# A four-layer kernel: the second batch's 50 rounds of balancing move from DVE to ACT and PE

## The reference

```python
def sinkhorn_log(logits, num_iters=50, tau=0.1):      # logits: one 4x4 matrix for each token
    Z = logits / tau
    def step(carry, _):
        u = -logsumexp(Z + v[..., None, :], axis=-1)
        v = -logsumexp(Z + u[..., :, None], axis=-2)
    (u, v), _ = scan(step, (0, 0), length=50)
    return exp(Z + u[..., :, None] + v[..., None, :])
...
H_res = (1 - g) * I + g * sinkhorn_log(H_res_logits)
x_mixed = einsum('btij,btjc->btic', H_res, x_streams)
ffn = x_mixed + y * softmax(H_post_logits)            # y = (x weighted by softmax(H_pre_logits)) @ W_branch
```

## Time and profile before

| | |
|---|---|
| median of 3 runs | 1462.56 us (1456.24 to 1465.91) |
| the profiled execution | 1467.78 us |
| its span in the trace | 1466.1 us |
| busy: PE / DVE / ACT / POOL | 1113.0 / 871.3 / 577.3 / 320.6 us |
| granted PE clock, mean | 0.868 |
| piece B + C + D + E | 155 + 125 + 125 + 156 us |

### The profile page before, as it was taken

How to read it: one execution, slowest core, us unless ns; L and a number is a source line. 1 busy time by engine, 2 the same in 40 slices (tenths; PEclk the granted TensorE clock), 3 DMA queues, 4 the chain that set the end, 5 groups by cost and what they waited for, 6 DMA issues and landing times.

```text
span 1466.1 us, 20210 instructions
## 1 busy us (share of the span) xinstructions
PE 1113.0 (76%) x7526; PEld 456.1 (31%) x7526; DVE 871.3 (59%) x1773; ACT 577.3 (39%) x785; POOL 320.6 (22%) x514
## 2 busy tenths in 40 slices
PE   2769999895788639746555457878788988898887
PEld 1444444342233314312312111222222233333332
DVE  4212222003666679886888988657758577746663
ACT  2413333000554435126113246574445555434452
POOL 1114444004841102001011043700010032111220
PEclk9869999997899859677776768998879999999999
DMA  3421220003210001100200111411002110210100
GB/s 130 144 87 45 85 65 22 0 0 94 65 29 18 12 1 55 34 6 20 62 13 22 56 53 36 138 29 31 17 27 74 50 32 23 77 54 28 53 18 29
DMA packets 53590, 67.14 MB, mean 46 GB/s; under 512 B 9494, under 2 KB 43412, under 8 KB 53488
## 3 DMA queue, kind: packets, MB, share of 16 engines
q1 hardware_dynamic: 49516, 55.95, 12.5%
q0 software_dynamic: 3984, 9.98, 2.4%
HBM read 46.82 MB, written 18.82 MB: 45 GB/s over the span
## 4 chain that ended last, share of the span: by engine, by line
PE 36%; DVE 31%; ACT 5%; issue 4%; SPq 1%; DMA 1%; ACTq 0%; DVEq 0%
DVE w_mx L1388 13%; PE w_banks L653 10%; PE w_po L1303 9%; PE w_banks L1285 4%; PE w_banks L1257 4%; DVE w_region L1875 3%; PE w_banks L1245 2%; ACT w_pr L1331 2%; DVE w_region L1872 2%; DVE w_region L1853 2%; DVE w_region L1870 2%; PE w_banks L1313 2%; PE w_banks L1539 1%; DVE w_region L1868 1%; DVE w_region L1866 1%
## 5 line engine op out<-in xcount | busy, mean ns | idle before, releaser
L1388 DVE TENSOR_REDUCE w_mx<-w_banks 128x2 f32<-128x1024 f32 (+3 forms) x352 | 377.1, 1087 | 195.6 <-PE w_banks L1257 194.0
L1331 ACT ACTIVATE w_pr<-w_banks 128x1024 f32<-128x1024 f32 (+1 forms) x312 | 315.1, 1013 | 429.3 <-PE w_banks L1285 427.9
L1370 POOL TENSOR_SCALAR_AFFINE_SELECT w_pr<-w_pr 128x512 f32<-128x512 f32 (+1 forms) x184 | 104.7, 569 | 561.5 <-ACT w_pr L1331 561.3
L1285 PE MATMUL w_banks<-w_qs,w_ks 49*128 49x512 f16 (+7 forms) x832 | 137.1, 354 | 91.1 <-DVE w_mx L1388 60.0
L1257 PE MATMUL w_banks<-w_ks,w_qs 48*128 48x512 f16 (+7 forms) x832 | 144.8, 361 | 40.9 <-DVE w_mx L1388 23.1
L1303 PE MATMUL w_po<-w_pr,w_vz 128*17 128x512 f32 (+7 forms) x1152 | 155.1, 565 | 12.7 <-ACT w_ou L1353 12.7
L78 PE MATMUL f_pp<-xt,sl_region 128*128 128x512 f16 x672 | 149.1, 382 | 3.5 <-POOL sl_region L492 3.5
L1245 PE MATMUL w_banks<-mask_half,ident_half 64*128 64x128 bf16 (+1 forms) x768 | 67.0, 254 | 37.2 <-DVE w_mx L1388 16.8
L78 PEld LDWEIGHTS f_pp<-xt,sl_region 128*128 128x128 f16 x672 | 65.1, 98 | 84.8 <-issue 5.6
L466 DVE TENSOR_TENSOR sl_region<-sl_region,f_pp 128x512 f32<-128x512 f32 x28 | 19.3, 688 | 121.3 <-ACT sl_region L481 121.3
L1285 PEld LDWEIGHTS w_banks<-w_qs,w_ks 49*128 49x128 f16 (+1 forms) x832 | 41.8, 99 | 138.9 <-issue 57.5
(11 more groups left out here) (223 smaller groups left out, 1533.6 us busy)
## 6 DMA issues: line engine op xcount, KB each, us to landing
stack_scratch<-sl_region SPq DMA_DIRECT2D x102, 128.0 KB
w_qs<-stack_scratch SPq DMA_DIRECT2D x96, 96.0 KB, 2.3
sl_region<-in_L_gu SPq DMA_DIRECT2D x14, 512.0 KB
w_stage<-in_L_w POOLq DMA_DIRECT2D x36, 128.0 KB, 2.4
sl_region<-in_L_down SPq DMA_DIRECT2D x14, 256.0 KB
stack_scratch<-p_qk SPq DMA_DIRECT2D x24, 128.0 KB
w_ks<-stack_scratch SPq DMA_DIRECT2D x32, 96.0 KB, 2.6
bw_stage<-in_L_w SPq DMA_DIRECT2D x4, 640.0 KB, 6.0
```

Of the source, the lines that this page charges most:

```text
L1285: mm = pe.matmul(g.banks.pair_at(f)[:, half, at:at + T - q0], g.ks[base:base + self.rows + 1, k_slot, k_place, j * P:(j + 1) * P], g.qs[ba ...
L1331: act.activation(g.probs.at(self.pr_fill[s])[:, :, 0:width], g.banks.pair_at(self.s_fill[s])[:, :, 0:width], ACT.Exp, scale=self.a.scale). ...
L1370: pool.affine_select(out=diagonal, in_=diagonal, compare_op=ALU.is_ge, fill=0.0, base=0, pattern=pattern, channel_multiplier=-1).then_inc( ...
L1388: dve.tensor_reduce(out, g.banks.pair_at(self.m_fill[m])[:, :, 0:heads * keys].rearrange("q h (p k) -> q h p k", k=keys), AX.X, ALU.max).t ...
```

## The change

`s1` becomes a `LogStreams`. The first batch's `s0` stays as it was. For `s1` the 64 columns are turned so that a partition is one of the 64 (tile, entry) pairs, for two halves of the tokens: `h_e` and `h_l` are 128 x 64. The logarithms of the matrices stay in a PSUM bank. A half round, of which there are 100, is four ticks: ACT takes exponents of the bank (L1965 in the new kernel, 128x64), PE multiplies them by a 128x128 table of ones, so that every entry gets the sum of its row or column (L1939, a single-precision matmul of 64 columns), ACT takes the logarithm of that (L1969, 128x64), and PE adds minus a tenth of it to the bank (L1943, the same size). 100 half rounds are 200 matmuls and 200 activations and one more exponent at the end; two transposes lead in and two lead out. Each tick waits for the one before. The bank of the logarithms and the one of the sums are held through the whole balancing; they are the first two of the seven, which is one pair.

After each Sqrt and each Silu the kernel now loads a table set that holds exponent and logarithm; the program has 35 table loads where it had 32, and none of them lies between the exponents and logarithms of the balancing.

The cuts between pieces move too. `s0` does 100 of its steps in piece B and 200 in piece C (before 180 and 120). `s1` does 10 half rounds in piece C (before 60 steps, which is 20 half rounds), 60 in piece D (before 240 steps and the mixing), and the last 30 with the mixing in piece E, ahead of what stood there: the output projection, norm and projections of batch 1 for layer 2 and the routed ffn now come behind the end of `s1` in the same strand. Line numbers of the new kernel are two higher than before up to the balancing.

```diff
...
         if t == 11:
             act.wait_ge(self.centred.sem, self.centred.at + 2)
-            act.activation(g.h_mix[:, :, :], g.h_mix[:, :, :], ACT.Exp, scale=self.INV_TAU).then_inc(self.exped.sem, 1)
-            act.activation(g.h_pp[:, :, :], g.h_pp[:, :, :], ACT.Exp).then_inc(self.exped.sem, 1)
+            self.exponents(act)
...
+class LogStreams(Streams):
+    def __init__(self, g, b, xn, w24, wb, base, gate, norm, weights, sums):
+        super().__init__(g, b, xn, w24, wb, base, gate, norm, weights)
+        self.sums = sums
+        s, self.halves = g.signals, 2 * self.ITERS
+        self.spread = s.take("h_spread", 1)
+        self.entries, self.totals = s.take("h_entries", self.halves + 1), s.take("h_totals", self.halves)
+        self.logs, self.taken = s.take("h_logs", self.halves), s.take("h_taken", self.halves)
+        self.gathered = s.take("h_gathered", 1)
+        self.gate_at = self.bal_at + 4 * self.halves + 2
+        self.mix_at = self.gate_at + 3
+        self.ticks = range(self.mix_at + NI * 4 + 1)
+    def rounds(self, signals):
+        return None
+    def plan(self, t):
+        super().plan(t)
+        banks = self.g.banks
+        if t == self.bal_at - 1:
+            self.fills["logs"] = banks.fill(self.entries, self.halves + 1, (self, self.gate_at - 2))
+            self.fills["totals"] = banks.fill(self.logs, self.halves, (self, self.gate_at - 4))
+        if t == self.gate_at - 1:
+            self.fills["back"] = banks.fill(self.done, 12, (self, self.gate_at + 1))
+    def pe(self, pe, t):
+        super().pe(pe, t)
+        g, banks = self.g, self.g.banks
+        if t == self.bal_at - 1:
+            pe.wait_ge(self.centred.sem, self.centred.at + 2)
+            banks.free(pe, self.fills["logs"])
+            for low in (0, 64):
+                mm = pe.matmul(banks.at(self.fills["logs"])[low:low + 64, 0:64],
+                               g.h_mix[low:low + 64, :, :].rearrange("p t n -> p (t n)"), g.ident[low:low + 64, low:low + 64],
+                               start=True, stop=True)
+            mm.then_inc(self.spread.sem, 1)
+            banks.free(pe, self.fills["totals"])
+        k, hop = divmod(t - self.bal_at, 4)
+        if 0 <= k < self.halves and hop == 1:
+            pe.wait_ge(self.entries.sem, self.entries.at + k + 1)
+            pe.matmul(banks.at(self.fills["totals"])[:, 0:64], self.sums[:, k % 2, :], g.h_e[:, :],
+                      start=True, stop=True).then_inc(self.totals.sem, 1)
+        if 0 <= k < self.halves and hop == 3:
+            pe.wait_ge(self.logs.sem, self.logs.at + k + 1)
+            pe.matmul(banks.at(self.fills["logs"])[:, 0:64], self.sums[:, 2, :], g.h_l[:, :],
+                      start=False, stop=True, skip_group_check=True).then_inc(self.taken.sem, 1)
+        if t == self.gate_at - 1:
+            banks.free(pe, self.fills["back"])
+            pe.wait_ge(self.entries.sem, self.entries.at + self.halves + 1)
+            for low in (0, 64):
+                mm = pe.matmul(banks.at(self.fills["back"])[low:low + 64, 0:64], g.h_e[low:low + 64, :],
+                               g.ident[low:low + 64, low:low + 64], start=True, stop=True)
+            mm.then_inc(self.gathered.sem, 1)
+    def exponents(self, act):
+        act.activation(self.g.h_pp[:, :, :], self.g.h_pp[:, :, :], ACT.Exp).then_inc(self.exped.sem, 2)
+    def act(self, act, t):
+        super().act(act, t)
+        g, banks = self.g, self.g.banks
+        k, hop = divmod(t - self.bal_at, 4)
+        if t >= self.bal_at and (k < self.halves and hop == 0 or t == self.gate_at - 2):
+            if k == 0:
+                act.wait_ge(self.spread.sem, self.spread.at + 1)
+            else:
+                act.wait_ge(self.taken.sem, self.taken.at + k)
+            act.activation(g.h_e[:, :], banks.at(self.fills["logs"])[:, 0:64], ACT.Exp, scale=self.INV_TAU)\
+                .then_inc(self.entries.sem, 1)
+        if 0 <= k < self.halves and hop == 2:
+            act.wait_ge(self.totals.sem, self.totals.at + k + 1)
+            act.activation(g.h_l[:, :], banks.at(self.fills["totals"])[:, 0:64], ACT.Ln).then_inc(self.logs.sem, 1)
+    def balance(self, dve, k):
+        pass
+    def weigh(self, dve):
+        g = self.g
+        dve.wait_ge(self.gathered.sem, self.gathered.at + 1)
+        dve.tensor_scalar(g.h_mix[:, :, :], g.banks.at(self.fills["back"])[:, 0:64].rearrange("p (t n) -> p t n", t=NI),
+                          g.h_gt[:, 1:2], None, ALU.mult).then_inc(self.done.sem, 1)
...
-        cut = s0.bal_at + 180
+        cut = s0.bal_at + 100
...
-        s1 = Streams(g, 1, sl[:, 1], w24, wb, base24[:, :], gate[:, :], n11, [])
+        s1 = LogStreams(g, 1, sl[:, 1], w24, wb, base24[:, :], gate[:, :], n11, [small.done()], sums)
         s1.begins_after = [(n11, n11.ticks[-1])]
-        cut1 = s1.bal_at + 60
+        cut1, cut2 = s1.bal_at + 40, s1.bal_at + 280
...
-               [some_of(s1, cut1, s1.ticks[-1] + 1)], [all_of(split2)]],
+               [some_of(s1, cut1, cut2)], [all_of(split2)]],
...
-        merge([[body_of(a20)], [all_of(o11), all_of(n21), all_of(p21), all_of(r20), lead_of(a21)], [all_of(split3)]],
+        merge([[body_of(a20)], [some_of(s1, cut2, s1.ticks[-1] + 1), all_of(o11), all_of(n21), all_of(p21), all_of(r20),
+                                lead_of(a21)], [all_of(split3)]],
...
+    at = np.arange(P)
+    out["sums"] = np.stack([at[:, None] // 4 == at // 4, (at[:, None] // 16 == at // 16) & (at[:, None] % 4 == at % 4),
+                            -0.1 * np.eye(P)], axis=1).astype(f)
```

More of the change, by code:

```diff
@@ L44 @@
 PR_UNITS = 6
+TABLES = "natural_log_exp_and_others"
 def wait_pos(eng, sem, value):
@@ L691, in act @@
             act.activation(self.g.sd[:, 1, :], self.g.sd[:, 0, :], ACT.Sqrt).then_inc(self.std.sem, 1)
+            act.preload_act_table_set(TABLES)
         c = t - 8
@@ L1674, in __init__ @@
         self.centred, self.exped = s.take("h_centred", 2), s.take("h_exped", 2)
-        self.balanced = s.take("h_balanced", 6 * self.ITERS)
+        self.balanced = self.rounds(s)
         self.pre, self.turned, self.hi, self.lo = s.take("h_pre", NI * 4), s.take("h_turned", 1), s.take("h_hi", 1), s.take("h_lo", 1)
@@ L1683, in __init__ @@
         self.fills = {}
+    def rounds(self, signals):
+        return signals.take("h_balanced", 6 * self.ITERS)
     def cost(self, t):
@@ L1762, in act @@
             op.then_inc(self.posted.sem, 1)
+    def exponents(self, act):
+        g = self.g
+        act.activation(g.h_mix[:, :, :], g.h_mix[:, :, :], ACT.Exp, scale=self.INV_TAU).then_inc(self.exped.sem, 1)
+        act.activation(g.h_pp[:, :, :], g.h_pp[:, :, :], ACT.Exp).then_inc(self.exped.sem, 1)
     def silu(self, act, pair):
@@ L1836, in dve @@
             dve.wait_ge(done.sem, done.at + 11)
-            dve.wait_ge(self.balanced.sem, self.balanced.at + 6 * self.ITERS)
-            dve.tensor_scalar(g.h_mix[:, :, :], g.h_mix[:, :, :], g.h_gt[:, 1:2], None, ALU.mult).then_inc(done.sem, 1)
+            self.weigh(dve)
         elif t == self.gate_at + 2:
@@ L1855, in dve @@
                                          op0=ALU.mult, op1=ALU.add).then_inc(self.mixed.sem, 1)
+    def weigh(self, dve):
+        g = self.g
+        dve.wait_ge(self.balanced.sem, self.balanced.at + 6 * self.ITERS)
+        dve.tensor_scalar(g.h_mix[:, :, :], g.h_mix[:, :, :], g.h_gt[:, 1:2], None, ALU.mult).then_inc(self.done.sem, 1)
     def balance(self, dve, k):
@@ L2037, in weave @@
     g.st, g.mv, g.sd = sb("st", [P, NI, 6], F32), sb("mv", [P, NI, 2], F32), sb("sd", [P, 3, NI], F32)
-    g.swap = sb("swap", [P, P], F32)
+    g.swap, sums = sb("swap", [P, P], F32), sb("sums", [P, 3, P], F32)
     g.rank = sb("rank", [P, 8], F32)
@@ L2055, in weave @@
     g.h_ss, g.h_rr, g.h_gt = (view(region, at, (n,), F32) for at, n in ((5872, 4), (5876, 4), (5880, 3)))
+    g.h_e, g.h_l = view(region, 5888, (64,), F32), view(region, 5952, (64,), F32)
     wo1, w24 = view(tables, 0, (2, 2, D), F16), view(tables, 1024, (2, KC, 24), F16)
@@ L2085, in weave @@
                                    (g.rank[:, :], ins["rank"].partition_broadcast(P)), (g.swap[:, :], ins["swap"]),
+                                   (sums[:, :, :], ins["sums"]),
                                    (col3[:, :], ins["L3_qk_bias"]), (v_row3[:, :], ins["L3_v_bias"].partition_broadcast(P)),
```

## The result

| | before | changed |
|---|---|---|
| median of the runs | 1464.24 us (1456.24 to 1467.43) | 1595.30 us (1592.96 to 1598.78) |
| ratio, 95% interval | | 1.0906 [1.0854, 1.0958] |
| profiled execution, span, mean clock | 1467.78, 1466.1 us, 0.868 | 1592.96, 1591.3 us, 0.828 |
| pieces B, C, D, E, F | 155, 125, 127, 154, 176 us | 139, 152, 157, 236, 172 us |

Pieces are measured here from the first of a stage's transposes (L968, now L970) to the next stage's. In the changed kernel these come late in piece E, so D ends with the 70th half round.

A forecast was written before the change was run, and what follows sets the result against it. DVE was taken to bound the balancing stretches, with the two-engine chain late next. Terms -10 + 20 + 5 + 19 + 48 = +82 us, set against the median 1462.6, gave 1545; predicted 1540 us, range 1475 to 1600.

The forecast's parts named there:

- The half round, 1.64 us: Four chain ticks: two activations of 0.22 us, two matmuls of 0.47, hand-overs of 0.10 and 0.03; bounds 1.0 and 2.3.
- Other work between its steps: Pieces D and E: PE's 58.5 us less 18.6 hidden plus 6 for ACT in D; attention ticks 24 us in E.
- Piece B, -10: 80 DVE steps, 23 us, leave piece B; PE then leads its second half; -9 us there, bounds 0 and -17.
- Piece C, +25: The 80 steps come to a stretch 87% DVE, +20 us (12 to 23); ten half rounds replace 60 steps, +5.
- Piece D, 144: 60 half rounds of 98 us plus PE's partly hidden other work and attention exponents: 144 us against 125, +19.
- Piece E, 73 + 31 + 100: 30 half rounds with 16 attention ticks 73 us, mixing 31, remaining attention ticks and other work 100: 204 against 156, +48.
- Queues, banks, table loads at nothing: POOL's splits in E, up to 8 us late, the held PSUM pair and three more table loads of 1.29 us: counted as nothing.
- Hiding (1): Rival: the chain hides beside other work and PE gets its full clock back, 1430 us; chance 0.08.
- A short matmul (2): Rival: matmuls of 0.23 to 0.30 us, most other work hidden, B and C cancelling, about 1465 us; chance 0.08.
- The low clock (3): Rival: PE mostly waits, so its clock stays low; half round 2.06 us, about 1605; chances 0.05 over 1600, 0.17 for 1565-1600.
- Alternating table sets (4): Rival: exponent and logarithm come from different table sets, costing 256 us in the balancing; chance under 0.01.
- The signs: Chain stretch 225 to 245 us, half rounds 1.64 apart; wrong if 1.1 or less, E's last third much under 100, C not growing.

The follow-up runs named there:

- experiment 1: Changed kernel with the second batch balancing on DVE as before, in the change's new places: 1484.85 us, ratio 1.014 against the kernel before.
- experiment 2: Changed kernel with its chain in places near the old ones, none in piece E: 1596.33 us, ratio 1.0907 against the kernel before.
- experiment 10: Changed kernel without the logarithm and subtraction of each half round, matrices unbalanced: 1500.40 us, ratio 1.0241 against the kernel before.
- experiment 7: Kernel before with two PSUM banks held unused through the second batch's balancing, which stays on DVE: 1467.77 us, ratio 1.0043.
- experiment 4: Kernel before with the second batch's 300 balancing steps left out, same written order: 1422.00 us, ratio 0.9722.

## Why the prediction was right, and where its sizes were off

- **Mechanism.** Right. DVE was relieved and what was late next was the chain (experiments 1, 2 and 10). The time, 1595, lies in the range, but only 5 us below its upper end, which was drawn for a half round of 2.2 us or the low clock. It is not in the 1490 to 1565 that had 0.62 but in the 1565 to 1600 that had 0.17. The forecast, 1540, was 55 us too low. Against the profiled execution's span it is +125 us where the sum had +82.
- **The half round, 1.64 us.** This term was too small. Without other work it was 2.00 us, with 0.69 for the matmul at the low clock, almost the 0.68 that the prediction had worked out for that clock. I took 0.47, "between the ends, because the clock of these pieces lies between". The mean was 0.60 (60.4 + 59.7 over 200). That is 26 us. The hand-over from ACT to PE was 0.06, not 0.10: 8 back. ACT's 0.22 was right. What I missed is that the clock would stay low although PE is busy 79% of the chain: I read 0.72 from a stretch in which PE did other things, and counted on a busier PE to raise it. The stretch from 716 to 740 ran at 0.50, all of it at 0.60, and the same places without a chain at 0.66 (experiment 1).
- **Other work between its steps.** 84 us of the 267, where the sum had 74 (238 less 164), at a clock of 0.72. In D it was 51 us (the sum: 58.5 - 18.6 + 6 = 46), in E 30 (24). The term for ACT was the one too small: in D its chain operations came 15 us late in all, where the sum had 6. Together the chain took 29 us more than the 21 + 144 + 73 of the sum.
- **Piece B, -10.** It was -16, at the good bound, with the clock at 0.94 in its second half instead of 0.84. **Piece C, +25.** It was +28: the head +20 as forecast, and 24 instead of 21 us for ten half rounds.
- **Piece D, 144.** It took 157. **Piece E, 73 + 31 + 100.** It took 86 + 35 + 115. The third part wasn't the chain's: experiment 1 has 119 there. PE had 85.2 us of work in it where I had 79.6, at a busy share of 75%. I had named 76% as one end and taken a value towards F's 85%; the stretch kept the share it had.
- **F unchanged.** 172 us against 176. **Queues, banks, table loads at nothing.** That was nearly so: the banks cost 6 us (experiment 7), the pair of loads inside the chain 2 us. The next activation began 1.29 us after the start of the second load, as in the earlier trace rows. The Trainium skill's drain of 1.38 us (ScalarE: Activation LUTs, "What ACT_TABLE_LOAD costs") is in neither. POOL's splits (60 us) found room in the third part.
- **The sum of the misses.** Chain +29, mixing +4, third part +15, B -6, F -4, pieces before B and after F +5: +43, which is 125 - 82.
- **The rivals.** Hiding (1) is refuted: without any second balancing the kernel gains 42 us (experiment 4), and the chain fills gaps only in the small. A short matmul (2) exists, in half precision, and gave the half round of 1.10 us; but the time fell to 1528, not 1465. The better clock and the better hiding that (2) counted on did not come: the clock was 0.59, and 100 half rounds took 200 us, not 110. The low clock (3) came true in part: a free half round of 2.00 us and a mean clock of 0.60. Its 1605 is nearer to the result than the forecast's 1540, and it deserved more than its 0.22. Its reason, that PE mostly waits, is not what the rows show: PE is busy 79% of the chain. Alternating table sets (4) did not come: one pair of loads in 200 activations, and that pair is another stage's.
- **The signs.** The stretch of the chain was 266 us from the first to the last of its matmuls, outside the 225 to 245 given, and a free half round 2.00 us instead of 1.64. The 0.22 us of the activations, the waits of PE and ACT for each other, DVE under a third busy in D and the pieces from F on came as said. None of the three signs of being wrong showed.
- **What stays open.** How long the chain would be at full clock: the fillers reached 0.83. With all its matmuls at the 0.43 us of the full clock instead of the mean 0.60, an estimated 34 us would go. PE's other work between them would be shorter too, by how much no run shows. In what way the new places lose their 21 us, beyond the rest of E, I did not take apart.

## What to carry to other kernels

Before moving a serial loop off a busy engine, multiply its steps by the length of one hop, at the slow clock that such a loop may run at, and compare with what taking it away altogether could bring: here 200 hops of 1.0 us against 42 us. A chain over two in-order engines costs its length plus most of the other work that is written between its steps: here 84 us, for 91 of PE and 37 of ACT. It hides only where pieces smaller than its gap stand beside it. Where a price depends on a clock, take the sum at either level of it first, since a stretch of the old kernel needn't show the clock of the new pattern.

## What the runs showed of the hardware

- A single-precision matmul with a 128x128 table and 64 columns is two records and took 0.69 us at the low clock, 0.43 at the full one; in half precision one record of 0.235 at the low clock. Its table is loaded again for each record (the 100 matmuls of L1943 have 200 loads of 0.28 us).
- With short matmuls, 119 of the 200 behind 0.31 us of idle time, the granted clock over the chain was 0.60, though PE was busy 79% of it. A filler in one of the two gaps of a half round made it 0.62, larger ones in both 0.83. I had not expected the first to bring so little and the second so much.
- A hop costs little in signals: 0.03 us from PE to ACT and 0.06 from ACT to PE.
